# Causal staircase of the self-attention chunks: second matmul on TensorE against an add in PSUM on VectorE

## The reference, cut to what matters

```python
# q from x, k and v from the context and from x (L1_xattn)
# scores of a query over 6404 context keys and over 1024 token keys;
# of the token keys only those not behind the query count
probs = softmax(where(visible, q @ k.T * HD ** -0.5, -inf))
out = (probs @ v) @ Wout + bout
```

## Time and profile before

| | |
|---|---|
| time, median of 3 runs | 3363.9 us (3363.48 to 3366.98) |
| the profiled execution | 3358.68 us, span 3356.9 us |
| PE busy | 3165.0 us, 94% |
| ACT busy | 2569.8 us, 77% |
| DVE busy | 349.4 us, 10% |
| POOL busy | 201.5 us, 6% |
| mean granted TensorE clock | 0.953 of full speed |
| share of the chain that ended last | PE 91%, DVE 3%, ACT 1% |
| the chain's two largest lines | L1618 37%, L1638 32% |

### The profile page before, as it was taken

The page is one execution under the profiler, slowest core; times in us unless marked ns, Lnnn a source line. Parts: engine busy times, 40 slices in busy tenths (PEclk is TensorE's granted clock), DMA queues, the critical chain, the costliest instruction groups (busy, mean ns, idle before and its releaser), DMA issues.

```text
span 3356.9 us, 59763 instructions
## 1 busy us (share of the span) xinstructions
PE 3165.0 (94%) x18587; PEld 1193.6 (36%) x18587; DVE 349.4 (10%) x952; ACT 2569.8 (77%) x2979; POOL 201.5 (6%) x715
## 2 busy tenths in 40 slices
PE   6679999999989799999999998969999999999988
PEld 3322222222233522322323224645632222222256
DVE  4410000000022500000000001342210000000021
ACT  3379999999933399799798994322289999999932
POOL 2000000000000000000000000010000000000000
PEclk9889999999979989899899997989999999999979
DMA  7711111111130011011010112101001111111110
GB/s 191 200 34 37 37 37 36 37 37 37 37 91 0 14 33 37 30 37 38 29 37 31 37 37 65 33 30 35 27 28 37 37 37 37 37 37 37 35 29 28
DMA packets 147807, 145.72 MB, mean 43 GB/s; under 512 B 17800, under 2 KB 101244, under 8 KB 147724
## 3 DMA queue, kind: packets, MB, share of 16 engines
q1 hardware_dynamic: 141840, 142.57, 14.0%
q10 hardware_dynamic: 5884, 2.08, 0.3%
HBM read 115.21 MB, written 29.57 MB: 43 GB/s over the span
## 4 chain that ended last, share of the span: by engine, by line
PE 91%; DVE 3%; issue 1%; SPq 1%; ACTq 1%; ACT 1%; POOL 1%; DMA 0%; DVEq 0%; POOLq 0%
PE PS L1618 37%; PE PS L1638 32%; PE PS L626 5%; PE PS L610 5%; PE PS L612 2%; PE PS L845 2%; PE PS L833 1%; PE PS L1468 1%; PE PS L1640 1%; PE PS L1478 1%; SPq L1111 1%; PE PS L1598 1%; PE PS L1682 1%; PE PS L1683 0%; PE PS L1604 0%
## 5 line engine op out<-in xcount | busy, mean ns | idle before, releaser
L1408 ACT ACTIVATE probs<-PS 128x1024 f32<-128x1024 f32 (+1 forms) x2496 | 2279.6, 1465 | 109.4 <-PE PS L1638 59.6
L1618 PE MATMUL PS<-probs,vr 128*32 128x512 f32 (+1 forms) x9984 | 1338.3, 609 | 1.5 <-DVE accs L1842 1.5
L1638 PE MATMUL PS<-qs,kr 35*128 35x512 f32 (+1 forms) x4992 | 1160.9, 500 | 29.1 <-issue 27.6
L1638 PEld LDWEIGHTS PS<-qs,kr 35*128 35x128 f32 x4992 | 480.2, 186 | 1340.0 <-ACT probs L1408 1222.2
L1268 POOL COPY vr<-vs 128x72 f32 (+1 forms) x624 | 157.8, 253 | 2834.5 <-PE PS L1618 2474.3
L1618 PEld LDWEIGHTS PS<-probs,vr 128*32 128x32 f32 x9984 | 198.3, 108 | 319.3 <-issue 181.2
L1842 DVE COPY accs<-PS 128x512 f32<-128x512 f32 x12 | 8.3, 692 | 2385.6 <-PE PS L1604 2385.6
L653 ACT ACTIVATE probs<-PS 128x512 f32<-128x512 f32 x96 | 57.4, 598 | 130.2 <-PE PS L610 71.4
L653 ACT ACTIVATE accs<-PS 128x512 f32<-128x512 f32 x96 | 57.3, 597 | 120.6 <-PE PS L610 63.2
L610 PE MATMUL PS<-xT,wide 128*128 128x512 f32 x256 | 124.9, 607 | 0.7 <-ACT xT L339 0.7
L626 PE MATMUL PS<-wide,accs 128*128 128x128 f32 x768 | 91.6, 281 | 5.0 <-DVE kf L685 5.0
(11 more groups left out here) (272 smaller groups left out, 1214.1 us busy)
## 6 DMA issues: line engine op xcount, KB each, us to landing
kr<-key_pieces SPq DMA_DIRECT2D x1248, 64.0 KB
key_pieces<-kparts SPq DMA_DIRECT2D x36, 288.0 KB, 4.5
kr<-mask_strips SPq DMA_DIRECT2D x624, 4.0 KB
key_pieces<-probs SPq DMA_DIRECT2D x32, 288.0 KB, 4.6
vs<-values SPq DMA_DIRECT2D x2, 3672.0 KB, 15.0
values<-v_next SPq DMA_DIRECT2D x9, 432.0 KB, 5.1
wide<-in_L_ffn_w SPq DMA_DIRECT2D x28, 128.0 KB, 2.1
values<-probs SPq DMA_DIRECT2D x8, 432.0 KB, 5.4
```

The lines of the kernel that those rows point to most:

```text
L1408: sc.activation(prob[n % RING][:, :, q0:], PS[:, bank:bank + 2, q0:], ACT.Exp, scale=SCALE).then_inc(p_ready, 1)
L1618: last = te.matmul(PS[32 * j:32 * j + 32, 7, q0:], vr[s.buf(c)][:, at_v:at_v + 32], prob[(n + j // 2) % RING][:, j % 2, q0:], start=fresh, ...
L1638: last = te.matmul(o, kr[b][own, p, :], qs[own, T8 // 2 * s.hh + p, 512 * s.qh + q0:512 * s.qh + 512], start=True, stop=not late)
```

## The change

The second product leaves PE. In its place DVE adds the staircase (`stair`, 0 or -1e30, bf16) to the diagonal block of both heads of a group, reading and writing PSUM, after `s_ready` of the group. A new semaphore `s_cut` counts these adds, and for the late chunks ACT waits for it instead of `s_ready`. There are 64 adds of 128 partitions x 2 x 128. Everything else, the order of the chunks and the three pairs of banks too, stays.

```diff
+    def cut(self, c):
+        return c >= FULL + 4 * self.qh
+    def cuts(self, c, p):
+        return 16 * (self.w % NSW) + 4 * (c - FULL - 4 * self.qh) + p + 1
...
-                        act.wait_ge(s_ready, i * (2 * BODY) + (n + 1))
+                        if s.cut(c):
+                            act.wait_ge(s_cut, s.cuts(c, p))
+                        else:
+                            act.wait_ge(s_ready, i * (2 * BODY) + (n + 1))
...
-                                last = te.matmul(o, kr[b][own, p, :], qs[...], start=True, stop=not late)
-                                if late:
-                                    last = te.matmul(o[:, 0:P], ident_b[:, :], stair[:, :], start=False, stop=True)
+                                last = te.matmul(o, kr[b][own, p, :], qs[...], start=True, stop=True)
...
                 for s in SWEEPS[4 * a:4 * a + 4]:
+                    for c in range(FULL + 4 * s.qh, s.n):
+                        for p in range(4):
+                            n, q0 = s.groups + 4 * c + p, s.seen(c)
+                            diagonal = PS[:, 2 * (n % TC):2 * (n % TC) + 2, q0:q0 + P]
+                            dve.wait_ge(s_ready, n + 1)
+                            v.tensor_tensor(diagonal, diagonal, stair[:, :].unsqueeze(1).to_broadcast([P, 2, P]), ALU.add).then_inc(s_cut, 1)
                     dve.wait_ge(left_used, s.w + 1)
                     v.tensor_copy(accs[:, s.hh, 512 * s.qh:512 * s.qh + 512], PS[:, 7, :]).then_inc(acc_ev, 1)
```

More of the change, by code:

```diff
@@ L259, in flamingo_decoder @@
         p_ready = sem("p_ready")
+        s_cut = sem("s_cut")
         pv_done = sem("pv_done")
@@ L1627, in scores @@
                         b, q0 = s.buf(c), s.seen(c)
-                        late = c >= FULL + 4 * s.qh
                         if g == 0:
@@ L1637, in scores @@
                                 o = PS[:, 2 * (n % TC) + e, q0:]
-                                last = te.matmul(o, kr[b][own, p, :], qs[own, T8 // 2 * s.hh + p, 512 * s.qh + q0:512 * s.qh + 512], start=True, stop=not late)
-                                if late:
-                                    last = te.matmul(o[:, 0:P], ident_b[:, :], stair[:, :], start=False, stop=True)
+                                last = te.matmul(o, kr[b][own, p, :], qs[own, T8 // 2 * s.hh + p, 512 * s.qh + q0:512 * s.qh + 512], start=True, stop=True)
                             last.then_inc(s_ready, 1)
```

## The result

The changed kernel takes 3291.44 us (median of 4 runs, 3287.56 to 3294.31) against 3364.01 of before (4 runs, 3363.48 to 3366.98): a ratio of 0.978, 95% interval 0.9765 to 0.9799, 72.6 us less. The profiled execution took 3293.15, span 3291.4.

What follows compares the result with a forecast made beforehand. PE was taken to bound the late stretches, with ACT waiting; 53.6 us from the stretches plus 15.8 from the clock made 69.4, taking 3363.9 to 3294.5, stated as 3294, range 3280 to 3322.

Steps and rivals of the forecast that it cites:

- lost company of the half-height scores: Late steps on PE: full-height products between paired scores stop them running together, 1.06 us a step beside the products' 0.64.
- The stretches: Four late stretches, first late score to next sweep: fall from 101.6 to 48.0 us, a gain of 53.6.
- The add: DVE's staircase add in late chunks: 0.42 us each, with zero and 0.69 as ends.
- The add hidden in the ring: Loop of three PSUM bank pairs: with the add, under ACT's pace at 512 columns, later than ACT in the last two chunks.
- No fall of the clock: PE's clock through and behind late stretches: stays at 1.00, so the next sweeps' ordinary work gains another 15.8 us.
- The first rival: PE's clock falls all the same, from the thin 128 chunk: gain only 44.5 us, 3319; chance 0.27.
- The rule of the Trainium skill on idle gaps: PE's clock should fall only with long idle gaps; if only idleness counted, the sum would lack the 15.8 us.
- The rival "no pairing": Late scores on PE stay in single file without the product, so only 20.5 us is gained: 3343; chance 0.04.
- The rival on the other side: Slower than before: the bank ring with DVE bounds late steps, from an add of 2.1 us on; 3386 at 2.8; chance 0.03.
- Key loads: Loads for late chunks: 3.9 us fits in 5.1 plus a value block, about a microsecond or two spare; cost nothing.
- one of the prediction's signs of being wrong: Late stretches: the prediction is wrong if PE waits for a key load in them.

Runs made afterwards that it cites:

- e2: The kernel before, all products still on PE but both score matmuls of a group first, then both products: 3306.62 us, ratio 0.9819.
- e7: The kernel before, old order, each product only on the 64 rows of its score's half, half the staircase left out: 3292.52 us, ratio 0.9788.
- e1: The kernel before without the second product and without an add, so no staircase at all: 3290.67 us, ratio 0.9773.
- e3: The changed kernel with PE's product back in the 256 and 128 chunks, the add kept in 512 and 384: 3341.24 us, ratio 0.9923.
- e4: The changed kernel with PE's product back in the 512 and 384 chunks, the add kept in 256 and 128: 3313.37 us, ratio 0.9846.
- e9: The changed kernel with each DVE add done three times in a row, same result: 3336.52 us, ratio 0.9909 against the kernel before.
- e10: The changed kernel with each DVE add done four times in a row, same result: 3370.65 us, ratio 1.0019 against the kernel before.
- e8: The changed kernel run once more, unaltered, on the chip of the repeated-add runs: 3290.32 us, ratio 0.9789 against the kernel before.

## Why the prediction was right

It was right, 3291.4 against 3294, and in the main by its own steps; two of its terms agree better than they should.

- The lost company of the half-height scores: forecast from one late step at 1.06 us a step beside 0.64 for the products. e2 and e7 show that standing between the scores is the larger part: 9.7 of 13.6 us a stretch come back by order alone. In the 512 steps, where the clock is 1.00 in all three kernels, the order gives 1.07 (3.36 to 2.29) and the move 0.46 (2.29 to 1.83, where ACT is the bound); in the narrow ones part of the 9.7 is the low clock of before. That 1.07 meets the 1.06 of the forecast is partly luck. By e2 the lost company is 0.86 a step (twice 0.43), for a pair ahead of a full-height product takes 0.43 and not 0.33; the other 0.21 comes from the two products now following each other. The sum of both terms was read from one whole step, so the total did not suffer. What the Trainium skill (TensorEngine Tiling (Array Packing), Key Properties) says of a drain at a change of tiling mode was not told apart from the plain fact that a full-height matmul needs both halves, nor from its late weights: the product's weight load starts 0.43 us behind the score (1367.52 to 1367.95, before), while in an ordinary step all four score loads are done within 0.30 us (from 1406.13). No run here separates the three; 0.43 behind a pair against 0.34 with half the height (e2, e7) is all that the height adds there.
- The stretches: 48.0 us forecast, 47.2 measured. The steps of 1.83, 1.62, 1.38 and 1.17 came out at 1.84, 1.70, 1.32 and 1.05 on average. For 384 columns the first step still waits for exponentials of the chunk before; for the narrow two the loop was reckoned 0.06 to 0.12 too long, perhaps since hand-overs and matmul ends were rounded up; no run tests that. The errors have opposite signs and in part cancel, so 47.2 is nearer to 48.0 than the single steps are.
- The add: taken at 0.42 from a row that does not write PSUM, measured at 0.43 on average, and 0.40 with the overlap of two in a row taken out (25.4 us / 64). Writing PSUM costs DVE little or nothing extra here (0.43 against the row's 0.415, whose second operand is another).
- The add hidden in the ring: shown by e1, 0.43 us a stretch.
- No fall of the clock, 15.8 us: 16.8 measured. That the narrow chunks decide between these kernels is shown by e3 and e4. What in them decides stays open: e2 kept all its products there and the clock stayed at 1.00, e9 had none and it fell. The first rival (the clock falls all the same, 3319) had 0.27 and did not come.
- The rule of the Trainium skill on idle gaps (TensorE: Matmul & The Clock Gate, HAM oscillation), weighed in the prediction: before, and in e3, the clock fell with PE busy throughout (13.60 of 13.60 us in e3), so idleness in the records was not needed. The ends of matmuls are modelled, so short gaps could hide in them. In e9, where PE did idle, the clock fell too.
- The rival "no pairing" (3343): out by the change itself, where four 384-column scores take 0.62 us (1372.19 to 1372.81), and by e7.
- The rival on the other side had the wrong price. It put the turning point at an add of 2.1 us by the loop of banks alone. The term that was missing is DVE's own time for two groups a step; with it the point is about 1.7, and e10 stands on it. At 0.43 neither is near, so the forecast did not suffer.
- Key loads: none bound a stretch of the profiled execution (11.80, 11.80, 11.81, 11.80). But one of the prediction's signs of being wrong, PE waiting for a key load, did occur once in e8 and once in e1, at 0.2 to 0.3 us. The forecast had a microsecond or two to spare there, with narrow steps of 1.38 and 1.17; they came at 1.32 and 1.05, and from the first to the last issue SP takes 1.82 us (1376.22 to 1378.04), not 1.78. The price is far below what the timing can tell.

## What to carry to other kernels

Look at who runs beside an instruction before pricing it: two half-height matmuls that run side by side lose each other when a full-height one is put between them. In the wide chunks putting the order right brought more than twice what it then brought to take the full-height ones away (1.07 against 0.46 us a step, the latter up to ACT's pace). If the product has to stay on PE, put it behind the pair; that alone was worth 1.8%. When work moves to an idle engine, check two bounds, the loop through the buffers and the engine's own time per step, since the second overtakes the first as the work grows. And when a stretch gets shorter, look again at the loads that it had hidden.

## What the runs showed of the hardware that was not expected

- Matmuls of 35 rows (f32) and of 64 rows (bf16) took turns in each half of the array, and the two halves kept in step, with the second matmul of each half adding into the bank of the first (e7: 0.87 us for eight matmuls; four scores alone take 0.66).
- The clock fell in a kernel whose PE had nothing but its ordinary matmuls in the stretch, with idle time between them (e9, first sweep: 1.00 until the 128 chunk, then 0.63 and 0.53), and did not fall in one with every product still on PE (e2: 1.00 through 15.67 us).
- A DVE operation in the same PSUM columns that PE wrote and ACT reads next costs 0.42 to 0.44 us back to back for 128x256, nearly what one that writes SBUF takes (0.415 in the earlier trace rows).
